# Chunked attention on one core: scores and the product with values side by side on TensorE, the output projection one step earlier

## The chip, the cores and the metric

The kernel runs on one core of one Trainium2 chip. The metric is the device time of one execution in microseconds (us). The kernel before took 1947.82 us, the median of 3 runs (1942.81 to 1955.28). The other seven cores do nothing.

## What is computed

The context `ctx` (32 batches of 256 channels by 2048 tokens) is projected into queries, keys and values, all three from the same tensor. Attention stays inside chunks of 64 tokens, with 8 heads of 32 channels. Then come the output projection, the mask, the residual `x` and a normalisation over the 2048 tokens of each channel:

```
qh, kh, vh = proj(ctx, W)                     # heads of 32, chunks of 64
scores = qh . kh * scale (+ NEG where masked)
attn   = softmax(scores)                      # over the 64 keys of the chunk
out    = (attn . vh) @ W_out.T + b_out
out    = out.transpose * masks + x
out    = (out - mean) * rsqrt(var + 1e-5)     # over the 2048 tokens
```

All arithmetic is float32. The large projections split each operand into a high and a low part (`ctx_hi`, `ctx_lo`, `w_hi`, `w_lo`) and add three products.

## The kernel before, in words

A *block* is 512 tokens of a batch, so there are 4 blocks in a batch and 128 in all. Each of five engines runs its own program, written out by hand: a function `step(p)` with p counting up, in which each operation works on a block at a fixed distance from p. So block p+2 is projected while block p+1 has its scores made, block p-1 is multiplied with the values and block p-2 goes through the output projection. Engines meet only at semaphores. Within an engine everything runs in the written order; an instruction that waits holds up all that stands behind it.

For one block the work is:

- SP (the queue that issues all DMAs) loads `ctx_raw` (four buffers), `mask_all` (six) and `x_raw` (two).
- ACT makes `ctx_hi` (`split_ctx`, L458), POOL `ctx_lo` (`low_ctx`, L565).
- TensorE projects keys, queries (`project_k`, `project_q`, L313) and values (`project_v`, L347), each in two halves that use the two banks of `proj_bank` in turn. ACT empties the banks (`keys` L500, `queries` L491, `values` L508). All projections, the output's too, share these two banks, so each half waits until the half before it in its bank is out.
- POOL turns the mask into rows of 0 or a large negative number (`masked_keys`, L587), and ACT lays them into the four score banks (`lay_negatives`, L470, two halves). Only when both halves lie there may the scores of the block be added on top.
- TensorE makes the scores with 128 matmuls of 32 rows by 64 columns (`scores`, L386). DVE takes the row maximum (L646) and subtracts it (L650, into `prob`, which frees the score banks). ACT takes the exponentials in two halves (L478), DVE sums them (L657) and takes reciprocals (L665), POOL multiplies (`divide`, L557, two halves).
- DVE turns the probabilities in 32x32 squares in one instruction (`turn`, L673), and SP puts them in place with eight DMAs of 128 KB (`move_probs`, L256). These eight wait for the whole turn. TensorE multiplies by the values with 128 matmuls of 64 rows by 32 columns (`probs_times_v`, L419).
- ACT and DVE split the attention output (`high_attention` L485, `low_attention` L680), TensorE projects it (`project_out`, L370, two halves), DVE adds bias and multiplies by the mask (`output`, L691), POOL adds `x` (`add_residual`, L575), DVE takes statistics (L700), and after four blocks the batch is normalised by ACT and POOL and stored.

The order inside a step on TensorE is: scores(p+1), keys(p+2), queries(p+2), first half of the output projection (p-2), product with values (p-1), second half of the output projection (p-2), values(p+2).

Of the kernel before, what the change touches and what calls it, by code (L numbers as in the profile page):

```python
# [14 lines left out]
HALVES = C // P  # L15
ROWS = P // DH
BLOCK = 512
BLOCKS = T // BLOCK
# [32 lines left out]
def attention_kernel(nc, x, ctx_in, mask, w_in_t, b_in, w_out_t, b_out, out):  # L51
    stack = ExitStack()
    with stack:
# [110 lines left out]
        def there(n):  # L164
            return 0 <= n < ALL
# [15 lines left out]
        def periods(step):  # L181
            for p in range(-3, ALL + 4):
                step(p)

        @block.sync
        def _(sp):
# [85 lines left out]
            def step(p):  # L272

                move_values(p + 1)
                if p >= -2:
                    load_ctx(p + 6)
                if there(p + 2):
                    sp.wait_ge(q_proj, 2 * (p + 2) + 1)
                if p >= -1:
                    load_mask(p + 3)  # L280
                if there(p + 2):
                    sp.wait_ge(q_proj, 2 * (p + 2) + 2)
                if p >= 3:
                    load_x(p - 1)
                move_probs(p)

                if p == ALL + 2:
                    for n in range(p - 7, ALL):
                        store(n)
                elif p < ALL + 2:  # L290
                    store(p - 7)

# [6 lines left out]
        def _(pe):  # L299
# [16 lines left out]


            def project_k(n, f):
                if not there(n):
                    return  # L320
                if f == 0:
                    pe.wait_ge(ctx_hi_done, 2 * (n + 1))
                    pe.wait_ge(ctx_lo_done, 2 * (n + 1) - 1)
                    if n == 0:
                        pe.wait_ge(ctx_lo_first, 1)
                wait(pe, v_f_done, 2 * (n - 1) + f + 1 if n else 0)
                project_qk(n, f, k_proj, C)
# [7 lines left out]
            def project_v(n, f):  # L335
                if not there(n):
                    return
                if there(n - 4):
                    pe.wait_ge(y_done, 2 * (n - 4) + f + 1)
                else:  # L340
                    pe.wait_ge(q_f_done, 2 * n + f + 1)
                for t in range(2):
# [9 lines left out]
            def project_out(m, f):  # L352
                if not there(m):
                    return
                if f == 0:
                    if m == 0:
                        pe.wait_ge(dve_const, 5)
                    pe.wait_ge(o_hi_done, m + 1)
                if there(m + 4):
                    pe.wait_ge(q_f_done, 2 * (m + 4) + f + 1)  # L360
                elif there(m + 3):
# [11 lines left out]

            def scores(n):
# [5 lines left out]
                pe.wait_ge(seeded, 2 * (n + 1))  # L380
                for c in range(CPB):
# [20 lines left out]

            def probs_times_v(n):
                if not there(n):
# [6 lines left out]
                wait(pe, o_lo_done, n)  # L411
                pe.wait_ge(moved[n % MOVES], 128 * (n // MOVES + 1))
                for c in range(CPB):
                    for r in range(ROWS):
# [17 lines left out]
            def step(p):  # L432
                met(PIECE_WAITS)
                scores(p + 1)
                project_k(p + 2, 0)
                project_k(p + 2, 1)
                project_q(p + 2, 0)
                project_q(p + 2, 1)
                if p == -1:
                    output_bias()  # L440
                project_out(p - 2, 0)
                probs_times_v(p - 1)
                project_out(p - 2, 1)
                project_v(p + 2, 0)
                project_v(p + 2, 1)

            periods(step)

        @block.scalar
        def _(act):  # L450
# [71 lines left out]

            def step(p):
                keys(p + 2, 0)
                split_ctx(p + 3, 0)
                keys(p + 2, 1)
                split_ctx(p + 3, 1)
                queries(p + 2, 0)
                queries(p + 2, 1)
                exponentials(p + 1, 0)  # L530
                exponentials(p + 1, 1)
                lay_negatives(p + 2, 0)
                lay_negatives(p + 2, 1)
                high_attention(p - 1)
                values(p + 2, 0)
                if p == ALL + 2:
                    for n in range(p - 7, ALL):
                        normalise(n)
                elif p < ALL + 2:
                    normalise(p - 7)  # L540
                values(p + 2, 1)

# [3 lines left out]
        def _(pool):  # L546
# [54 lines left out]
            def step(p):  # L601
                if p < 0:
                    masked_keys(p + 2)
                low_ctx(p + 3, 0)
                low_ctx(p + 3, 1)
                if p >= 0:
                    masked_keys(p + 2)
                if p < ALL + 2:
                    normalise(p - 7)
                if there(p - 3) and (p - 3) % BLOCKS == BLOCKS - 1:  # L610
                    reciprocal_std((p - 3) // BLOCKS)
                if p == ALL + 2:
                    for n in range(p - 7, ALL):
# [9 lines left out]
        def _(dve):  # L623
# [103 lines left out]
            def step(p):  # L727
                less_maximum(p + 1)
                if p == -1:
                    output_bias()  # L730
                turn(p)
                statistics(p - 3)
                done = there(p - 3) and (p - 3) % BLOCKS == BLOCKS - 1
                if done:
                    mean_and_variance((p - 3) // BLOCKS)
                output(p - 2, 0)
                sum_up(p + 1, 0)
                output(p - 2, 1)
                sum_up(p + 1, 1)
                reciprocals(p + 1)  # L740
                low_attention(p - 1)
                if done:
                    mean_shift((p - 3) // BLOCKS)
                if p == ALL + 2:
                    normalise_last()
# [25 lines left out]
```

## Time and profile before

| what | value |
|---|---|
| median of 3 runs | 1947.82 us |
| profiled execution, span from first to last instruction | 1939.0 us |
| TensorE matmul busy | 1891.7 us, 98% |
| DVE busy | 1703.2 us, 88% |
| POOL busy | 1504.6 us, 78% |
| ACT busy | 1330.1 us, 69% |
| mean granted clock of TensorE | 0.991 |
| DMA engines, share of the span (main queue) | 74.2% |

The device time of the profiled execution itself is not listed apart from its span; the median of the three runs lies 8.8 us above that span. Times in the trace are counted from the start of the span. A row of the timeline gives the start and the length of an instruction (or of several merged, with x2 and so on), the engine, the line in the kernel and the tile it writes. In the chain of waits a row is a stretch of time and the work that filled it.

### The profile page before, as it was taken

How to read it: one execution, taken by the hardware profiler on the slowest of the kernel's cores; microseconds unless marked ns; L12 is line 12 of the kernel's file. 1: busy time of each engine (PE TensorE's matmuls, PEld its weight loads, DVE VectorE, ACT ScalarE, POOL GpSimd, SP SyncE). 2: the span in 40 equal slices, each digit the busy share in tenths (PEclk: the TensorE clock that was granted, in tenths of full speed). 3: DMA queues.
4: the chain of work that ended last, by engine and by line, in shares of the span. 5: the costliest groups of instructions: out<-in, count | busy, mean ns of one | idle time of the engine just before them, and what ended most of it. 6: DMA issues, size and time to landing. Idle time of an engine off the chain costs nothing.

```text
span 1939.0 us, 90624 instructions
## 1 busy us (share of the span) xinstructions
PE 1891.7 (98%) x40488; PEld 1608.1 (83%) x40488; DVE 1703.2 (88%) x1577; ACT 1330.1 (69%) x1792; POOL 1504.6 (78%) x1059
## 2 busy tenths in 40 slices
PE   7999999999999999999999999999999999999994
PEld 6888888888888888888888888888888888888882
DVE  4898889899999978998988999888899889989986
ACT  5667667767767766776777677677667767767762
POOL 4677778878888778878777887787778778778874
PEclk9999999999999999999999999999999999999997
DMA  5667778777777767777777777777777777777766
GB/s 171 159 181 215 218 206 224 215 218 223 212 220 222 213 196 217 222 215 215 221 219 212 221 222 214 222 210 215 212 221 219 215 217 216 222 209 222 208 176 195
DMA packets 242882, 409.60 MB, mean 211 GB/s; under 512 B 28992, under 2 KB 94784, under 8 KB 242496
## 3 DMA queue, kind: packets, MB, share of 16 engines
q1 hardware_dynamic: 242496, 403.82, 74.2%
q8 instruction: 320, 5.24, 1.2%
q14 instruction: 66, 0.54, 0.1%
HBM read 168.82 MB, written 67.11 MB: 122 GB/s over the span
## 4 chain that ended last, share of the span: by engine, by line
PE 96%; DVE 1%; issue 1%; ACT 1%; DMA 0%; POOL 0%; SPq 0%; DVEq 0%
PE proj_bank L313 38%; PE proj_bank L370 19%; PE proj_bank L347 19%; PE score_bank L386 11%; PE o_bank L419 9%; DMA b_cols<-b_in 0%; ACT prob L478 0%; ACT score_bank L470 0%; DVE squares L673 0%; SPq L256 0%; POOL prob L557 0%; DVE stats L700 0%; POOL y L575 0%; DMA prob_t<-squares 0%; DVE sums L657 0%
## 5 line engine op out<-in xcount | busy, mean ns | idle before, releaser
L557 POOL TENSOR_TENSOR prob<-prob,recip 128x1024 f32<-128x1024 f32 x256 | 482.0, 1904 | 46.5 <-DVE recip L665 46.5
L575 POOL TENSOR_TENSOR y<-y,x_raw 128x512 f32<-128x512 f32 x256 | 331.5, 1295 | 181.1 <-DVE y L691 181.1
L565 POOL TENSOR_TENSOR ctx_lo<-ctx_raw,ctx_hi 128x512 fp32r<-128x512 f32 x255 | 330.2, 1295 | 171.9 <-ACT ctx_hi L458 159.7
L500 ACT ACTIVATE k_f<-proj_bank,b_cols 128x512 f32<-128x512 f32 x256 | 176.4, 689 | 365.2 <-PE proj_bank L313 365.2
L646 DVE TENSOR_REDUCE row_max<-score_bank 128x32 f32<-128x2048 f32 x128 | 293.4, 2292 | 138.7 <-PE score_bank L386 138.7
L313 PE MATMUL proj_bank<-ctx_hi,w_hi 128*128 128x512 f32 x1024 | 337.1, 410 | 3.0 <-DVE ctx_lo L630 3.0
L313 PE MATMUL proj_bank<-ctx_hi,w_lo 128*128 128x512 f32 x1024 | 322.1, 396 | 0.7 <-issue 0.7
L313 PE MATMUL proj_bank<-ctx_lo,w_hi 128*128 128x512 f32 x1024 | 322.1, 396 | 0.0
L657 DVE TENSOR_REDUCE sums<-prob 128x16 f32<-128x1024 f32 x256 | 309.3, 1209 | 5.0 <-ACT prob L478 5.0
L650 DVE TENSOR_TENSOR prob<-score_bank,row_max 128x2048 f32<-128x2048 f32 x128 | 293.3, 2292 | 4.4
L673 DVE STREAM_TRANSPOSE squares<-prob 128x2048 f32<-128x2048 f32 x128 | 294.6, 2301 | 2.6 <-POOL prob L557 2.6
L478 ACT ACTIVATE prob<-prob 128x1024 f32<-128x1024 f32 x256 | 255.2, 1047 | 5.6 <-DVE prob L650 5.6
L491 ACT ACTIVATE q_f<-proj_bank,b_cols 128x512 f32<-128x512 f32 x256 | 176.4, 689 | 115.1 <-PE proj_bank L313 115.1
L470 ACT ACTIVATE score_bank<-neg_rows 128x1024 f32<-128x1024 f32 x256 | 251.3, 1016 | 0.0
L587 POOL TENSOR_SCALAR neg_rows<-mask_all 128x512 f32<-128x512 f32 x128 | 247.0, 1929 | 2.5 <-DMA mask_all<-mask 2.5
L691 DVE SCALAR_TENSOR_TENSOR y<-proj_bank,b_final,mask_all 128x512 f32<-128x512 f32 x256 | 190.3, 744 | 49.8 <-PE proj_bank L370 49.8
L313 PEld LDWEIGHTS proj_bank<-ctx_hi,w_lo 128*128 128x128 f32 x1024 | 194.0, 189 | 46.9 <-issue 1.0
L313 PEld LDWEIGHTS proj_bank<-ctx_lo,w_hi 128*128 128x128 f32 x1024 | 193.5, 189 | 45.2
L313 PEld LDWEIGHTS proj_bank<-ctx_hi,w_hi 128*128 128x128 f32 x1024 | 183.9, 189 | 46.5 <-issue 3.7
L386 PE MATMUL score_bank<-k_f,q_f 32*64 32x64 f32 x16384 | 214.7, 233 | 3.0 <-ACT score_bank L470 2.8
L386 PEld LDWEIGHTS score_bank<-k_f,q_f 32*64 32x64 f32 x16384 | 196.7, 130 | 21.3 <-issue 3.8
L419 PEld LDWEIGHTS o_bank<-prob_t,v_f 64*32 64x32 f32 x8192 | 169.8, 105 | 51.2 <-issue 51.2
(45 smaller groups left out, 3487.1 us busy)
## 6 DMA issues: line engine op xcount, KB each, us to landing
prob_t<-squares SPq DMA_DIRECT2D x1024, 128.0 KB
ctx_raw<-ctx SPq DMA_DIRECT2D x128, 512.0 KB, 4.8
x_raw<-x SPq DMA_DIRECT2D x128, 512.0 KB, 4.8
out<-y SPq DMA_DIRECT2D x128, 512.0 KB, 4.3
mask_all<-mask SPq DMA_DIRECT2D x128, 256.0 KB, 4.2
v_x<-v_f SPq DMA_DIRECT2D x256, 128.0 KB, 3.4
y<-w_in_t SPq DMA_DIRECT2D x1, 768.0 KB, 5.6
y<-w_out_t SPq DMA_DIRECT2D x1, 256.0 KB, 6.7
```

Source lines behind the costliest of these rows:

```text
L313: last = pe.matmul(proj_bank[:, f, :], w[:, h, col + f * P:col + (f + 1) * P], c[:, n % 2, h, :], start=(a == 0 and h == 0), stop=(a == 2 ...
L347: last = pe.matmul(proj_bank[:, f, t * C:(t + 1) * C], c[:, n % 2, h, tok:tok + P], w[:, h, 2 * C:3 * C], start=(a == 0 and h == 0), stop= ...
L370: last = pe.matmul(proj_bank[:, f, :], w[:, h, f * P:(f + 1) * P], o[:, m % 2, :, h, :], start=(a == 0 and h == 0), stop=(a == 2 and h == 1))
L386: last = pe.matmul(score_bank[f * CHUNK:(f + 1) * CHUNK, r, tokens], q_f[head, n % 2, f, tokens], k_f[head, n % 2, f, tokens], start=False ...
L419: last = pe.matmul(o_bank[r * DH:(r + 1) * DH, f, c * CHUNK:(c + 1) * CHUNK], values, prob_t[keys, :, r * CPB + c, :], start=True, stop=Tr ...
L557: pool.tensor_tensor(part, part, half(slots(recip[:, n % 2, :]), i), ALU.mult).then_inc(norm_done, 1)
L565: pool.tensor_tensor(ctx_lo[:, n % 2, :, tokens], ctx_raw[:, n % BLOCKS, :, tokens], ctx_hi[:, n % 2, :, tokens].bitcast(F32), ALU.subtrac ...
L575: pool.tensor_tensor(part, part, x_raw[:, m % 2, f, :], ALU.add).then_inc(added, 1)
L646: dve.tensor_reduce(row_max[:, :].rearrange("p (r c) -> p r c", c=CPB), scores_of, AX_X, ALU.max).then_inc(max_done, 1)
L650: dve.tensor_tensor(prob[:, n % 2, :, :, :], scores_of, slots(row_max[:, :]), ALU.subtract).then_inc(less_done, 1)
L657: dve.tensor_reduce(sums[:, i * SLOTS // 2:(i + 1) * SLOTS // 2], half(prob[:, n % 2, :, :, :], i).rearrange("p r c k -> p (r c) k"), AX_X ...
L673: dve.transpose(squares[:, :, :, :], prob[:, n % 2, :, :, :].rearrange("p r c (b j) -> p b (r c) j", j=SQ)).then_inc(turned, 1)
```

## The change

No instruction of arithmetic is added or removed; the steps are arranged anew.

- TensorE: one group of waits at the head of a step (context, queries and keys and laid rows, moved probabilities), then scores(p+1), product with values(p-1), keys(p+2), queries(p+2), values(p+2), and both halves of the output projection, now of block p-1. The banks are waited for accordingly.
- ACT: splitting of the context and of the attention output first; the first half of the mask rows is laid before the queries and exponentials, the second half after the values.
- POOL: the residual is added at the head of the step, ahead of `low_ctx` and `masked_keys`.
- DVE: `low_attention` right behind `turn`; the output of block p-1 at the end, behind the reciprocals.
- SP: the store first, then context, the eight moves, x, the values' move, the mask.
- The turn stays one instruction, and the eight moves still wait for all of it; only their order among themselves differs. Two steps at the end go.

```diff
         def periods(step):
-            for p in range(-3, ALL + 4):
+            for p in range(-3, ALL + 2):
                 step(p)
...
             def move_probs(n):
-                sp.wait_ge(turned, n + 1)
-                wait(sp, pv_done, n)
-                for f in range(HALVES):
-                    for a in range(2):
-                        for b in range(2):
+                wait(sp, pv_done, n)
+                sp.wait_ge(turned, n + 1)
+                for b in range(2):
+                    for f in range(HALVES):
+                        for a in range(2):
...
             def step(p):                       # SP
-                move_values(p + 1)
+                store(p - 7)
+                if there(p + 2):
+                    sp.wait_ge(k_proj, 2 * (p + 2) + 1)
                 if p >= -2:
                     load_ctx(p + 6)
-                if there(p + 2):
-                    sp.wait_ge(q_proj, 2 * (p + 2) + 1)
+                move_probs(p)
+                if p >= 3:
+                    load_x(p - 1)
+                move_values(p + 2)
                 if p >= -1:
                     load_mask(p + 3)
-                if there(p + 2):
-                    sp.wait_ge(q_proj, 2 * (p + 2) + 2)
-                if p >= 3:
-                    load_x(p - 1)
-                move_probs(p)
...
             def step(p):                       # TensorE
                 met(PIECE_WAITS)
+                context_ready(p + 2)
+                rows_ready(p + 1)
+                probs_ready(p - 1)
                 scores(p + 1)
+                probs_times_v(p - 1)
                 project_k(p + 2, 0)
                 project_k(p + 2, 1)
                 project_q(p + 2, 0)
                 project_q(p + 2, 1)
                 if p == -1:
                     output_bias()
-                project_out(p - 2, 0)
-                probs_times_v(p - 1)
-                project_out(p - 2, 1)
                 project_v(p + 2, 0)
                 project_v(p + 2, 1)
+                project_out(p - 1, 0)
+                project_out(p - 1, 1)
...
             def step(p):                       # ACT
+                split_ctx(p + 3, 0)
+                split_ctx(p + 3, 1)
+                high_attention(p - 1)
                 keys(p + 2, 0)
-                split_ctx(p + 3, 0)
                 keys(p + 2, 1)
-                split_ctx(p + 3, 1)
+                lay_negatives(p + 2, 0)
                 queries(p + 2, 0)
+                exponentials(p + 1, 0)
                 queries(p + 2, 1)
-                exponentials(p + 1, 0)
                 exponentials(p + 1, 1)
-                lay_negatives(p + 2, 0)
+                values(p + 2, 0)
+                values(p + 2, 1)
                 lay_negatives(p + 2, 1)
-                high_attention(p - 1)
-                values(p + 2, 0)
...
             def step(p):                       # POOL
                 if p < 0:
                     masked_keys(p + 2)
+                add_residual(p - 2, 0)
+                add_residual(p - 2, 1)
                 low_ctx(p + 3, 0)
                 low_ctx(p + 3, 1)
                 if p >= 0:
                     masked_keys(p + 2)
...
-                add_residual(p - 2, 0)
-                add_residual(p - 2, 1)
                 divide(p + 1, 0)
                 divide(p + 1, 1)
...
                 turn(p)                        # DVE
-                statistics(p - 3)
+                low_attention(p - 1)
+                statistics(p - 2)
...
-                output(p - 2, 0)
                 sum_up(p + 1, 0)
-                output(p - 2, 1)
                 sum_up(p + 1, 1)
                 reciprocals(p + 1)
-                low_attention(p - 1)
+                output(p - 1, 0)
...
+                output(p - 1, 1)
```

What a step of ACT looks like in the middle of the program, before (lines of the kernel before; `k_f`, `q_f`, `v_f` are keys, queries, values taken out of `proj_bank`):

```order
L500 ACTIVATE k_f<-proj_bank,b_cols 128x512 [waits rows_done,k_proj]
L458 ACTIVATE ctx_hi<-ctx_raw 128x2x256 [waits v_proj,ctx_loaded3]
L500 ACTIVATE k_f<-proj_bank,b_cols 128x512 [waits rows_done,k_proj]
L458 ACTIVATE ctx_hi<-ctx_raw 128x2x256
L491 ACTIVATE q_f<-proj_bank,b_cols 128x512 [waits q_proj] x2
L478 ACTIVATE prob<-prob 128x1024 [waits less_done] x2
L470 ACTIVATE score_bank<-neg_rows 128x1024 [waits less_done,neg_done]
L470 ACTIVATE score_bank<-neg_rows 128x1024
L485 ACTIVATE o_hi<-o_bank 128x1024 [waits out_proj,pv_done]
```

and the same stretch now:

```order
L491 ACTIVATE o_hi<-o_bank 128x1024 [waits out_proj,pv_done]
L506 ACTIVATE k_f<-proj_bank,b_cols 128x512 [waits rows_done,k_proj] x2
L476 ACTIVATE score_bank<-neg_rows 128x1024 [waits less_done,neg_done]
L497 ACTIVATE q_f<-proj_bank,b_cols 128x512 [waits q_proj]
L484 ACTIVATE prob<-prob 128x1024 [waits less_done]
L497 ACTIVATE q_f<-proj_bank,b_cols 128x512 [waits q_proj]
L484 ACTIVATE prob<-prob 128x1024 [waits less_done]
L514 ACTIVATE v_f<-proj_bank 128x512 [waits pv_done,v_proj] x2
L476 ACTIVATE score_bank<-neg_rows 128x1024
```

The first laying of the mask rows, with its wait for POOL (`neg_done`), has moved ahead of both queries and both exponentials. POOL's step, before:

```order
L565 TENSOR_TENSOR ctx_lo<-ctx_raw,ctx_hi 128x2x256 [waits ctx_hi_done] x2
L587 TENSOR_SCALAR neg_rows<-mask_all 128x512 [waits seeded,mask_loaded4]
L598 TENSOR_SCALAR y<-y,rstd,shift 128x512
L575 TENSOR_TENSOR y<-y,x_raw 128x512 [waits x_loaded0,y_done]
L575 TENSOR_TENSOR y<-y,x_raw 128x512 [waits y_done]
L557 TENSOR_TENSOR prob<-prob,recip 128x1024 [waits recip_done]
```

and now:

```order
L563 TENSOR_TENSOR prob<-prob,recip 128x1024
L581 TENSOR_TENSOR y<-y,x_raw 128x512 [waits x_loaded0,y_done]
L581 TENSOR_TENSOR y<-y,x_raw 128x512 [waits y_done]
L571 TENSOR_TENSOR ctx_lo<-ctx_raw,ctx_hi 128x2x256 [waits ctx_hi_done] x2
L593 TENSOR_SCALAR neg_rows<-mask_all 128x512 [waits seeded,mask_loaded4]
L604 TENSOR_SCALAR y<-y,rstd,shift 128x512
```

The two additions of the residual now stand between the division and the mask rows. On SP a step now reads:

```order
L230 DMA out<-y 128x2x512 [waits z_done1,z_done0]
L194 DMA ctx_raw<-ctx 128x2x512 [waits ctx_lo_done,k_proj]
L256 DMA prob_t<-squares 32x1024 [waits turned,pv_done]
L256 DMA prob_t<-squares 32x1024 x7
L211 DMA x_raw<-x 128x2x512 [waits added]
L241 DMA v_x<-v_f 64x4x128 [waits pv_done,v_f_done]
L241 DMA v_x<-v_f 64x4x128
L203 DMA mask_all<-mask 128x512 [waits y_done]
```

The load of x, which stood ahead of the eight moves, is behind them.

## Rows read from the trace of the kernel before

**Rows 1.** Chain of waits, one step of TensorE: start us, us, what.
```profile
915.84 2.88 PE proj_bank L347 x24
918.72 1.59 PE score_bank L386 x92
920.30 5.77 PE proj_bank L313 x24
926.07 1.40 PE proj_bank L370 x6
927.48 1.41 PE o_bank L419 x91
928.89 1.58 PE proj_bank L370 x6
```

**Rows 2.** Timeline of DVE: start us, us, engine line operation tiles.
```profile
916.55 1.21 DVE L657 TENSOR_REDUCE sums<-prob 128x16 f32<-128x1024 f32 x1
917.86 0.35 DVE L665 RECIPROCAL recip<-sums 128x32 f32<-128x32 f32 x1
...
924.87 2.30 DVE L673 STREAM_TRANSPOSE squares<-prob 128x2048 f32<-128x2048 f32 x1
```

**Rows 3.** Timeline of ACT.
```profile
911.48 0.69 ACT L491 ACTIVATE q_f<-proj_bank,b_cols 128x512 f32<-128x512 f32 x1 [0.71 <-PE proj_bank L313]
912.06 2.00 ACT L478 ACTIVATE prob<-prob 128x1024 f32<-128x1024 f32 x2
913.96 1.96 ACT L470 ACTIVATE score_bank<-neg_rows 128x1024 f32<-128x1024 f32 x2
...
917.31 0.60 ACT L508 ACTIVATE v_f<-proj_bank 128x512 f32<-128x512 f32 x1 [0.44 <-PE proj_bank L347]
```

**Rows 4.** Timeline of POOL.
```profile
918.29 3.77 POOL L557 TENSOR_TENSOR prob<-prob,recip 128x1024 f32<-128x1024 f32 x2 [0.28 <-DVE recip L665]
923.22 2.67 POOL L565 TENSOR_TENSOR ctx_lo<-ctx_raw,ctx_hi 128x512 fp32r<-128x512 f32 x2 [1.17 <-ACT ctx_hi L458]
925.86 1.92 POOL L587 TENSOR_SCALAR neg_rows<-mask_all 128x512 f32<-128x512 f32 x1
...
929.08 1.29 POOL L575 TENSOR_TENSOR y<-y,x_raw 128x512 f32<-128x512 f32 x1 [0.54 <-DVE y L691]
```

**Rows 5.** Chain of waits at the end, last eight moves: first, last with landing, the product.
```profile
1909.42 0.51 SPq L256
...
1913.78 2.44 DMA prob_t<-squares
...
1916.35 1.67 PE o_bank L419 x96
```

**Rows 6.** Timeline of SP, the eight moves in the middle of the run.
```profile
928.97 6.20 SPq L256 DMA_DIRECT2D prob_t<-squares  x8
```

**Rows 7.** The page, DMA issues: KB each, us to landing.
```profile
x_raw<-x SPq DMA_DIRECT2D x128, 512.0 KB, 4.8
```

**Rows 8.** Chain of waits, two stretches in which TensorE stood still.
```profile
262.44 1.64 issue
...
703.69 2.60 issue
...
706.77 2.86 PE proj_bank L370 x6
```

**Rows 9.** Busy time by stretch: PE, PEld, DVE, ACT, POOL busy, clock, DMA share, GB/s.
```profile
265.00:266.00 1.00, 1.00 (x7) 0.83 (x6) 0.00 (x0) 0.56 (x1) 0.00 (x0) 1.00 0.32 74
...
706.00:707.00 1.00, 0.70 (x18) 0.53 (x18) 0.00 (x0) 0.13 (x1) 0.00 (x0) 0.50 0.04 16
...
712.00:713.00 1.00, 1.00 (x8) 1.00 (x8) 1.00 (x2) 0.77 (x2) 0.92 (x1) 0.76 0.85 197
```

**Rows 10.** Chain of waits: the scores of block 3, and those of block 127.
```profile
61.66 1.75 PE score_bank L386 x86
...
1888.91 1.59 PE score_bank L386 x93
```

More of the change, by code:

```diff
@@ L315, in project_qk, with context_ready @@
                 last.then_inc(proj, 1)
+            def context_ready(n):
+                if not there(n):
+                    return
+                pe.wait_ge(ctx_hi_done, 2 * (n + 1))
+                pe.wait_ge(ctx_lo_done, 2 * (n + 1) - 1)
+                if n == 0:
+                    pe.wait_ge(ctx_lo_first, 1)
             def project_k(n, f):
@@ L320, in project_k @@
                     return
[L321 to L326, printed above, removed]
+                if there(n - 4):
+                    pe.wait_ge(y_done, 2 * (n - 4) + f + 1)
+                else:
+                    wait(pe, v_f_done, 2 * (n - 1) + f + 1 if n else 0)
                 project_qk(n, f, k_proj, C)
@@ L337, in project_v @@
                     return
[L338 to L341, printed above, removed]
+                pe.wait_ge(q_f_done, 2 * n + f + 1)
                 for t in range(2):
@@ L358, in project_out @@
                     pe.wait_ge(o_hi_done, m + 1)
-                if there(m + 4):
-                    pe.wait_ge(q_f_done, 2 * (m + 4) + f + 1)
-                elif there(m + 3):
+                if there(m + 3):
                     pe.wait_ge(v_f_done, 2 * (m + 3) + f + 1)
@@ L372, in project_out, with rows_ready @@
                 last.then_inc(out_proj, 1)
-            def scores(n):
+            def rows_ready(n):
                 if not there(n):
@@ L380, in scores @@
                 pe.wait_ge(seeded, 2 * (n + 1))
+            def scores(n):
+                if not there(n):
+                    return
                 for c in range(CPB):
@@ L401, in open_banks, with probs_ready @@
                 last.then_inc(opened, 1)
-            def probs_times_v(n):
+            def probs_ready(n):
                 if not there(n):
@@ L412, in probs_times_v @@
                 pe.wait_ge(moved[n % MOVES], 128 * (n // MOVES + 1))
+            def probs_times_v(n):
+                if not there(n):
+                    return
                 for c in range(CPB):
@@ L523, in step @@
             def step(p):
+                split_ctx(p + 3, 0)
+                split_ctx(p + 3, 1)
+                high_attention(p - 1)
                 keys(p + 2, 0)
-                split_ctx(p + 3, 0)
                 keys(p + 2, 1)
-                split_ctx(p + 3, 1)
+                lay_negatives(p + 2, 0)
                 queries(p + 2, 0)
+                exponentials(p + 1, 0)
                 queries(p + 2, 1)
-                exponentials(p + 1, 0)
                 exponentials(p + 1, 1)
-                lay_negatives(p + 2, 0)
+                values(p + 2, 0)
+                values(p + 2, 1)
                 lay_negatives(p + 2, 1)
-                high_attention(p - 1)
-                values(p + 2, 0)
-                if p == ALL + 2:
-                    for n in range(p - 7, ALL):
+                if p == ALL + 1:
+                    for n in range(p - 6, ALL):
                         normalise(n)
-                elif p < ALL + 2:
-                    normalise(p - 7)
-                values(p + 2, 1)
+                else:
+                    normalise(p - 6)
             periods(step)
@@ L607, in step @@
                     masked_keys(p + 2)
[L608 to L613, printed above, removed]
+                if p < ALL + 1:
+                    normalise(p - 6)
+                if there(p - 2) and (p - 2) % BLOCKS == BLOCKS - 1:
+                    reciprocal_std((p - 2) // BLOCKS)
+                if p == ALL + 1:
+                    for n in range(p - 6, ALL):
                         normalise(n)
-                add_residual(p - 2, 0)
-                add_residual(p - 2, 1)
                 divide(p + 1, 0)
```

14 lines of the change are left out of this document (6 added, 8 removed).

## The prediction, made before the changed kernel was run

> **What bounds the kernel now.** I read the chain of waits first. In the middle of the run it never leaves TensorE: one step is values 2.88, scores 1.59, keys and queries 5.77, first half of the output projection 1.40, product with values 1.41, second half 1.58, in all 14.63 us without a gap [rows 1]. From the scores of block 3 to those of block 127 lie 124 steps and 1888.91 - 61.66 = 1827.25 us, so 14.74 a step [rows 10]; the 0.11 above 14.63 is a handful of stalls such as those of [rows 8]. What is left is 61.7 us ahead of them and 1939.0 - 1888.9 = 50.1 us behind. The timelines of the other engines come next, because the change rearranges who waits for whom: the reader should see there how long each link is.
>
> **TensorE's own work.** The step now has one stretch of small tiles instead of two. Re-entering the large matmuls costs 1.58 - 1.40 = 0.18 us [rows 1], and one of the two entries goes: 14.63 - 0.18 = 14.45. No row shows scores directly followed by the product with values; that seam costs between 0 (they are both small tiles) and about 0.18 (as dear as the entry seen). I take 0; it won't decide. The Trainium skill, TensorEngine Tiling (Array Packing), section Key Properties, says that a change of tiling mode drains the array; scores (32 by 64) to product (64 by 32) is such a change, and by it the sum would be 14.6 instead of 14.45. If nothing else waited, 124 steps would save 0.18 x 124 = 22 us.
>
> **Something else waits.** Three loops close once a step, through the other engines.
>
> *Loop of the mask rows.* POOL now does, in order: divide, two residual additions, `ctx_lo`, mask rows. ACT may not take out the queries or do the exponentials until it has laid the first half of those mask rows, and the exponentials lead back to the next division. From the end of the mask rows (call it M): laying one half 0.98 (1.96 for two), queries 0.58 to the next start, exponential 0.95 (913.96 - 912.06 = 1.90 for two), queries 0.58, exponential 1.00 [rows 3]; the second sum to its reciprocal 1.31, reciprocal to division 0.43 [rows 2, 4]; division 3.77, two additions 2.58, `ctx_lo` 2.67, mask rows 1.92 [rows 4]. Sum 16.77; two crossings between engines that these starts don't hold, about 0.05 each by the 0.08 between reciprocal and division, make 16.9 us. Before, the laying stood behind the exponentials, so the loop wasn't closed.
>
> *Where TensorE stands in it.* It reaches the values' projection at 1.59 + 1.41 + 5.77 = 8.8 us of its step [rows 1], but bank 0 is free only at M + 0.05 + 0.98 + 0.69 = M + 1.7. Values start there, the first half of the output projection at M + 4.8 (the values' bank is emptied after the second exponential, 4.15 + 0.60 [rows 3]), and the step ends at M + 4.8 + 2.8 = M + 7.6. With a step of 16.9, M lies at 16.9 - 7.6 = 9.3 and TensorE stands still from 8.8 to 11.0: 2.2 us in every step.
>
> *Loop of the moves.* From the start of the scores to the end of the turn took 927.17 - 918.72 = 8.45 us [rows 1, 2]; that order is unchanged on DVE. From the first of eight issues to the product that needed them it was 1916.35 - 1909.42 = 6.93 us when little else moved [rows 5]. Now the scores of the next step stand behind the same wait, so a step takes at least 8.45 + 6.93 = 15.4 us. Before, the product came later in the step and the moves were issued over a step early; nothing waited.
>
> *Loop of x.* Its load now follows the eight moves: 8.45, eight issues 5.0 (4.36 / 7 = 0.62 each) [rows 5], landing 4.8 [rows 7], two additions, `ctx_lo`, mask rows 7.2, then 7.6 to the end of a step. That is 33.1 us over two steps, 16.5 each. It is just short of the first loop, so whatever delays the scores soon delays x and with it M.
>
> **What the standstill does to the clock.** After 2.60 us of standstill, which began at 703.69, the granted clock was 0.50 at 706 and came back in the course of 712 [rows 8, 9]: 1.2 GHz instead of 2.4 for at least 6.5 us. Six large matmuls took 2.86 there against 1.40 to 1.58 [rows 1, 8]. After 1.64 us at 262 it stayed at 1.00 [rows 8, 9]. A standstill of 2.2 lies between the two, so I count it as even odds. If the clock falls, values and half of the output projection run at half speed and the step ends at M + 10.5 instead of M + 7.6, as 6.5 us at half speed lose about 3.3, of which 0.4 lay in waits between the halves. The end of the outputs then holds up POOL's additions by some 0.5. The next step has M 6.9 after its start and no standstill at the values, but its head waits for the moves (15.4), and its x lands 8.45 + 5.0 + 4.8 = 18.2 after its start where POOL is through with its division at 6.9 + 9.6 = 16.5 (M + 5.9 to the reciprocal by the links above, and 3.77): 1.7 more. Two steps are then 2 x 16.9 + 0.5 + 1.7 = 36.0, or 18.0 each, and the standstill that follows is 2.2 + 0.7 = 2.9, long enough to drop the clock again. So once it falls it keeps falling every second step. The Trainium skill, TensorE: Matmul & The Clock Gate, section HAM oscillation, describes this pattern, a wait in every round that puts the clock down each time; the row at 706 agrees for one wait, none here shows it repeated.
>
> **The sum.** I take the pairs with a fallen clock for three quarters of the steps and 16.9 for the rest: 0.75 x 18.0 + 0.25 x 16.9 = 17.7 us. The head: two early steps get longer by about 4 in all (scores of blocks 1 to 3 at 15.5 apart), 65.7. The tail keeps its chain of division, turn, moves, product, output and normalisation; a step fewer and one late output less may save up to 3, I keep 50.1. Together 65.7 + 50.1 + 124 x 17.7 = 2311 us of span. The median lay 8.8 above the span of the profiled execution, so 2320 us. In short, time = 125 + 124 x step. Splitting, keys, statistics and the store are moved too; all have over 1 us of slack beside a step of 17 and cost nothing, as DVE is busy 1703.2 / 128 = 13.3 us a step and ACT 1330.1 / 128 = 10.4. If POOL's loop were gone, DVE would be the one with little to spare.
>
> **Rivals.**
> - *The clock holds* (the 2.2 us behave like the 1.64): step 16.9, 125 + 2096 = 2221 us. For it: 2.2 is only 0.56 longer than a standstill that left the clock alone. Against: one fall is enough to make the next standstill 2.9 long. Chance 0.24.
> - *Moves and x cost more.* In the middle of the run the eight issues took 6.20 us rather than 5.0 [rows 6]. 1.2 more on x in every late step gives (36.0 + 1.2) / 2 = 18.6, and 2431 us; falls in each step would do the same. For it: the DMA engines were busy 74% of the span, and the moves end in a landing like any other. Against: in the new order little else is in flight during the moves. Chance 0.13.
> - *Only the moves bind.* If the mask rows come early enough, because part of POOL's work is shorter in company than the rows say, the step is 15.4, up to 16.4 with the 6.20: 2035 to 2160 us. It decides only if the mask-row loop shrinks by 1.5 us of 16.9. Chance 0.11.
> - *Faster than before.* The seam saved is real; it shows if the moves land within TensorE's own 14.45 us, that is if turn to product takes 14.45 - 8.45 = 6.0 instead of 6.93, and if ACT's laying isn't held (loop under 14.45, 2.4 below my sum). Then 61.7 + 50.1 + 8.8 + 124 x 14.45 = 1912 us. Against: each link of both loops is a measured length. Chance 0.04, 0.01 of it within 1% of the time before.
>
> **Chances and range.** Forecast case (step 17.2 to 18.1) 0.48. The range reaches from 2195, below the clock that holds, to 2425, the upper bound of the moves; it leaves out the last two rivals and a part of the dear moves. About 1% is what a measurement of this kernel can tell from no change. Slower by over 1% 0.96, within 1% 0.01, faster 0.03.
>
> **What would show it.** In the profile after: TensorE's busy share falls to some 85%; the first large wait on it is at the values' projection, on the queries taken out by ACT; ACT waits at L476 for POOL's mask rows; POOL is nearly without gaps from division to mask rows, and waits only for the reciprocals, with some wait for x; the granted clock has a mean of 0.8 to 0.9. If TensorE instead waits at the head of the step for the moves and nowhere else, the loop of the mask rows was overrated and the step is 15.4 to 16.4. If the step is 14.5, both loops were.

## The result, and the profile after

The changed kernel takes 2720.77 us (median of 4 runs, 2695.01 to 2730.98) against 1951.55 of the kernel before (4 runs): a ratio of 1.393, interval 1.387 to 1.399. The forecast was 2320, with a range up to 2425. The direction was right, the size was not: a step takes 20.98 us (scores of block 3 at 73.55, of block 127 at 2674.88, 124 steps) instead of the 17.7 forecast.

The page of the profile after, busy time by engine, the clock by slice, the queue that brings instructions, and the chain by engine:

```profile
PE 2156.2 (79%) x40488; PEld 1796.8 (66%) x40488; DVE 1756.9 (65%) x1577; ACT 1303.7 (48%) x1792; POOL 1472.0 (54%) x1059
...
PEclk8888888878888888888887888888898888888886
...
q8 instruction: 320, 5.24, 0.8%
...
PE 71%; issue 20%; DMA 4%; SPq 3%; DVE 1%; POOL 1%; ACT 0%; DVEq 0%; ACTq 0%
```

TensorE's busy share fell from 98% to 79%, and a fifth of the chain is "issue": time in which the engine waited for nothing that the profile shows. The head of one step of that chain and the whole of the next, where [rows 1] had a step without a gap (start us, us, what; lines of the changed kernel: 385 scores, 422 product, 308 keys and queries, 345 values, 366 output):

```profile
1306.59 1.52 PE score_bank L385 x91
1308.11 0.17 PE o_bank L422
1308.28 2.61 issue
1310.89 2.04 PE o_bank L422 x121
1312.93 0.72 PE proj_bank L308
1313.65 0.98 issue
1314.63 6.75 PE proj_bank L308 x23
...
1327.09 1.58 PE score_bank L385 x84
1328.67 0.79 PE o_bank L422 x53
1329.46 3.40 issue
1332.86 0.85 PE o_bank L422 x53
1333.70 7.32 PE proj_bank L308 x24
1341.02 2.84 PE proj_bank L345 x24
1343.87 2.78 PE proj_bank L366 x12
1346.65 1.52 PE score_bank L385 x91
```

The rows show a stop *inside* the product. It is not at the seam with the scores and not at the head of the step. It begins 0.17 us after the product's first matmul in one step and 0.79 in the next, and the two alternate through the run. By the records of the product in these stretches, 1 and 65 of the 128 matmuls had run. The step with the early stop has another one, of 0.98 us here, behind the first matmul of the keys, which is exactly 128 matmuls further on. The second step adds up: 19.56 us = 14.38 of work at full speed, 3.40 of stop, 1.55 more for keys and queries than their 5.77 in [rows 1], and 0.23 by which the product's two parts exceed 1.41. The 1.55 is the clock:

```profile
1332.00:1333.00 1.00, 0.14 (x18) 0.14 (x25) 1.00 (x1) 0.00 (x0) 1.00 (x2) 1.00 0.00 0
...
1334.00:1335.00 1.00, 1.00 (x5) 0.82 (x4) 1.00 (x1) 0.77 (x1) 1.00 (x2) 0.74 0.00 0
1335.00:1336.00 1.00, 1.00 (x4) 0.81 (x3) 1.00 (x2) 0.10 (x1) 1.00 (x1) 0.50 0.00 0
```

(busy time of PE, PEld, DVE, ACT, POOL, then granted clock, DMA share and GB/s, as in [rows 9]). After the standstill the clock goes to 0.50, 1.2 GHz. Over the run its mean is 0.84. The waits of the whole run, engine, line, what for, total us, times, longest:

```profile
ACT o_hi L491 <- PE o_bank L422: 853.9, 128, 9.0
PE o_bank L422 <- issue: 444.2, 126, 5.1
PE proj_bank L308 <- issue: 77.0, 63, 2.1
PE score_bank L385 <- DMA prob_t<-squares: 6.7, 17, 1.1
ACT score_bank L476 <- POOL neg_rows L593: 2.1, 1, 2.1
PE proj_bank L345 <- ACT q_f L497: 1.7, 1, 1.7
```

The stop comes in 126 of 128 products, 3.5 us each. What the prediction put first, ACT waiting for the mask rows and TensorE for the queries, is next to nothing: 2.1 and 1.7 us. For the moves TensorE waited 6.7 us at the scores.

### The profile page after: what moved, and what is told of

The parts are those of the page before. It is cut to its first block, busy times and chain, and to the rows that moved or that the text cites. A ratio compares the mean times of both kernels' runs of the same rounds, so it can differ in the third digit from the quotient of the medians.

```text
span 2723.3 us, 90494 instructions
## 1 busy us (share of the span) xinstructions
PE 2156.2 (79%) x40488; PEld 1796.8 (66%) x40488; DVE 1756.9 (65%) x1577; ACT 1303.7 (48%) x1792; POOL 1472.0 (54%) x1059
## 3 DMA queue, kind: packets, MB, share of 16 engines
q8 instruction: 320, 5.24, 0.8%
## 4 chain that ended last, share of the span: by engine, by line
PE 71%; issue 20%; DMA 4%; SPq 3%; DVE 1%; POOL 1%; ACT 0%; DVEq 0%; ACTq 0%
PE proj_bank L308 32%; PE proj_bank L345 12%; PE proj_bank L366 11%; PE o_bank L422 9%; PE score_bank L385 7%; DMA prob_t<-squares 3%; SPq L256 3%; POOL prob L563 0%; DVE squares L679 0%; DVE row_max L652 0%; SPq L194 0%; DMA b_cols<-b_in 0%; ACT score_bank L476 0%; DVE sums L663 0%; POOL ctx_lo L571 0%
## 5 line engine op out<-in xcount | busy, mean ns | idle before, releaser
L422 PE MATMUL o_bank<-prob_t,v_f 64*32 64x64 f32 x8192 | 260.7, 270 | 445.8 <-issue 441.9
L491 ACT ACTIVATE o_hi<-o_bank 128x1024 fp32r<-128x1024 f32 x128 | 131.0, 1023 | 853.9 <-PE o_bank L422 853.9
L308 PE MATMUL proj_bank<-ctx_hi,w_hi 128*128 128x512 f32 x1024 | 444.3, 512 | 79.9 <-issue 77.0
L422 PEld LDWEIGHTS o_bank<-prob_t,v_x 64*32 64x32 f32 x8192 | 199.6, 126 | 460.5 <-issue 460.5
L308 PE MATMUL proj_bank<-ctx_hi,w_lo 128*128 128x512 f32 x1024 | 397.6, 476 | 0.0
L308 PE MATMUL proj_bank<-ctx_lo,w_hi 128*128 128x512 f32 x1024 | 384.7, 462 | 0.0
L308 PEld LDWEIGHTS proj_bank<-ctx_hi,w_lo 128*128 128x128 f32 x1024 | 248.3, 242 | 156.8 <-issue 94.3
L308 PEld LDWEIGHTS proj_bank<-ctx_hi,w_hi 128*128 128x128 f32 x1024 | 242.5, 251 | 72.7 <-issue 21.5
L308 PEld LDWEIGHTS proj_bank<-ctx_lo,w_hi 128*128 128x128 f32 x1024 | 240.2, 235 | 63.6
L422 PE MATMUL o_bank<-prob_t,v_x 64*32 64x64 f32 x8192 | 241.5, 271 | 2.4 <-issue 2.4
```

Of the source, the lines that this page charges most:

```text
L308: last = pe.matmul(proj_bank[:, f, :], w[:, h, col + f * P:col + (f + 1) * P], c[:, n % 2, h, :], start=(a == 0 and h == 0), stop=(a == 2 ...
L422: last = pe.matmul(o_bank[r * DH:(r + 1) * DH, f, c * CHUNK:(c + 1) * CHUNK], values, prob_t[keys, :, r * CPB + c, :], start=True, stop=Tr ...
```

## The experiments

**Theory S**: scores and product in a row are 256 small matmuls and 256 weight loads in some 3 us. TensorE uses up its instructions faster than they arrive and stands still until the next piece of the program is there. The page has 320 packets and 5.24 MB of instructions on q8, 16.4 KB each. TensorE executes 2 x 40488 = 80976 matmuls and loads, 253 for each of those packets, so I take a piece as 256 instructions; the rest would be its waits for semaphores. That the stops of two neighbouring steps lie 64 matmuls, or 128 instructions, apart fits a step of 640 instructions: 320 packets for 128 steps are two and a half in each. **Rivals**: the moves of the probabilities (M), the change of tile shape at the seam (T), and the prediction's loops as the only cost.

The trace of the changed kernel also has the times of those packets. Set beside the stops of the chain above, with the times at which TensorE went on:

| packet of q8 lands | TensorE goes on | later by |
|---|---|---|
| 1309.75 | 1310.89 | 1.14 us |
| 1313.21 | 1314.63 | 1.42 us |
| 1331.38 | 1332.86 | 1.48 us |

So it is in the whole run: of the 189 stops over 0.5 us behind the start of the program, 188 end 1.0 to 1.7 us after such a packet has landed, with a median of 1.39, though there is a packet only every 8.5 us. The same holds for the four stops in the kernel before (1.33 to 1.51). That TensorE stood still until a piece of its program had come is thus shown, and the experiments show what makes the pieces late.

### One part alone: the product behind the scores, in the kernel before

```diff
                 scores(p + 1)
+                probs_times_v(p - 1)
                 project_k(p + 2, 0)
...
                 project_out(p - 2, 0)
-                probs_times_v(p - 1)
```

> The kernel before with one thing changed: on TensorE the product with values(p-1) stands right behind scores(p+1). Theory S (supply of instructions): 128 + 128 small matmuls with their 256 weight loads in a row use up TensorE's instructions faster than they arrive; it stops for 1.5 to 4.5 us inside the product in every step, the granted clock falls behind it, step 18.5 to 20.5 us, 2400 to 2650 us. Theory M (moves): nothing but the earlier need for the eight moves counts (turn to landing), step 15.4 to 16.5, 2030 to 2170 us, and the wait stands at the product's first matmul with the moves as releaser. Theory T (seam): a stop at the seam between 32*64 and 64*32 tiles, at the product's first matmul, the same in each step.

Measured 2557.5 us (e1), ratio 1.308 (1.289 to 1.326). The time is that of theory S, its mechanism is not in the rows:

```profile
PE o_bank L419 <- DMA prob_t<-squares: 404.7, 127, 5.1
...
1330.89 0.37 SPq L211
...
1336.09 5.30 DMA prob_t<-squares
1341.38 0.14 issue
1341.52 2.18 PE o_bank L419 x127
```

TensorE waits at the product's first matmul for the moves, 3.2 us in 127 steps. SP issues these only behind the load of x, which in the old order waits for the second half of the queries; the moves then land 5.3 us after the last issue. So this is M's place, at 19.3 us for this step (the product before began at 1322.20) where M said at most 16.5. The run shows that the adjacency alone costs 31% in the old surroundings. It says nothing on stops for instructions, which that wait would hide.

### Keys between scores and product, in the changed kernel

```diff
                 scores(p + 1)
-                probs_times_v(p - 1)
                 project_k(p + 2, 0)
                 project_k(p + 2, 1)
+                probs_times_v(p - 1)
...
-                high_attention(p - 1)
                 keys(p + 2, 0)
                 keys(p + 2, 1)
+                high_attention(p - 1)
```

> The changed kernel with the two key projections (12 + 12 instructions, 2.9 us) put between scores and product, and ACT's split of the attention output behind the keys. Theory S: the stops inside the product are gone or under 1 us, and what is left is the loop of the mask rows of the prediction: step 16.9 to 18.0, 2220 to 2360 us. Theory M: the wait for the moves is untouched, still 2650 to 2730 us. Theory T: two more seams with large tiles, 0.2 us each, and the stop gone with the seam, also 2220 to 2360: e4 tells it from S.

Measured 2271.0 us (e2), ratio 1.161 (1.156 to 1.167): 450 us came back from moving one group by 2.9 us. Its chain is the loop of x of the prediction, link by link:

```profile
1345.37 2.31 DVE squares L679
...
1353.22 5.30 DMA x_raw<-x
...
1361.18 2.48 POOL ctx_lo L571 x2
1363.66 1.90 POOL neg_rows L593
...
1367.27 3.23 PE proj_bank L345 x24
```

Between the turn and the landing lie the eight issues. Stops remain, but 188 us in 120 waits instead of 528 in 190 (all waits of PE's matmuls put down to "issue").

### Keys and queries between

The edit is the same with both queries ahead of the product too; ACT splits the attention output behind the exponentials, DVE behind the reciprocals.

> As e2, but keys and queries (5.8 us of large matmuls) between scores and product, and the attention output split behind the exponentials on ACT and behind the reciprocals on DVE. Theory S: no stop at all inside the product, step 16.9 to 18.0 by the loop of the mask rows, 2220 to 2360 us, at most 2% from e2. Theory M: 2650 us or more.

Measured 2479.6 us (e3), ratio 1.268 (1.259 to 1.277). A miss: stops fell further, to 90 us in 64 waits, but the product now comes 5.8 us later, the moves wait for it (`pv_done`), x waits behind the moves, and the loop of x is 18.8 us a step (scores at 1308.45 and, two steps on, at 1346.05). The stops are only one of the costs.

### The same program, 64 idle waits fewer at its head

```diff
-LEAD = 102
+LEAD = 38
```

> The changed kernel with 38 instead of 102 idle waits at the head of TensorE's program (64 instructions fewer, nothing else). In the changed kernel the stop begins 0.17 us behind the product's first matmul in one step and 0.79 in the next. Theory S: pieces of the program now end 64 instructions later in the work, so the stop begins some 0.35 us later, at 0.5 and 1.1 us; time 2650 to 2780 us. Theories M and T: the stop has nothing to do with the place in the program, it begins at 0.17 and 0.79 as before, time within 1%.

Measured 2565.9 us (e4): 5.7% less than the changed kernel, for removing waits that run once. It fell below the expected time. The chain of this run, one stop of each kind:

```profile
1334.78 0.97 PE o_bank L422 x64
1335.74 4.23 issue
...
1356.15 0.28 PE o_bank L422 x17
1356.43 4.64 issue
```

The stops begin behind 17 and 81 matmuls instead of 1 and 65. The distance of 64 stays and both have moved by 16 matmuls, 32 instructions. I had expected 64, or 0.35 us. The other runs with a changed LEAD agree that two idle waits count as one instruction: 64 fewer move the stop of the kernel before from behind matmul 111 of the product to behind 127 (e10 below), and 36 more move it by 9 matmuls between e14 and e13. That the place moves at all excludes T and M, which know nothing of the place in the program. What became cheaper is mainly the stop behind the first matmul of the keys: 77.0 us in 63 waits in the changed kernel, 2.4 in one wait here, while the stops in the product still take 419.5 of 444.2.

### The load on the DMA engines

```diff
-                sp.dma_start(out[... all 256 rows of the block ...])
+                sp.dma_start(out[bass.ds(batch, 1), 0:1, j * BLOCK:(j + 1) * BLOCK]...)
...
+                rows = P if n < MASKS else 1
-                sp.dma_start(mask_all[:, n % MASKS, :], ...)
+                sp.dma_start(mask_all[0:rows, n % MASKS, :], ...)
```

> The changed kernel without most of the two transfers that SP issues just ahead of the burst: the store of the result writes 2 KB instead of 512 KB per block, and masks behind the first six blocks load one row instead of 128 (the output is left out except for one row of each block). Everything else waits as before. Theory C (the pieces of TensorE's program queue behind the transfers on the same DMA engines): the stop inside the product shrinks from 3.6 us in the mean to under 2, time 2350 to 2520 us. Theory L (a piece simply takes long): the stop stays at 3.3 to 3.8 us and the time within 3% of the changed kernel.

Measured 2478.2 us (e5), 8.9% less than the changed kernel. The stops:

```profile
PE o_bank L423 <- issue: 263.4, 126, 3.6
```

That is 2.09 us each against 3.53, a little over the 2 I had named. Pieces of the program come later when the DMA engines are loaded. The packets themselves take as long as before (median 1.08 us against 0.98), and TensorE goes on as long after they land (1.39 in both), so it is their start that comes later. More than half of the stop stays without these two transfers.

### The mask rows late, x early, and both

```diff
-                lay_negatives(p + 2, 0)      # rows late: ahead of the queries ...
+                lay_negatives(p + 2, 0)      # ... now behind exponentials(p + 1, 1)
...
+                    load_x(p - 1)            # x early: ahead of ...
                 move_probs(p)
-                    load_x(p - 1)            # ... not behind
```

> e2 with the first laying of the mask rows back behind the exponentials on ACT. Theory of the prediction's loops: the loop of the mask rows is open, and the loop of x with it, as x only leads to the next step through those rows: step 14.8 to 15.8, 1960 to 2085 us. Rival (x alone sets the step of e2): 2230 us or more.

> e2 with the load of x issued ahead of the eight moves, nothing else. Prediction's loops: the loop of x is gone, that of the mask rows (16.9 us a step) stays, 2190 to 2240 us. Rival (x alone sets the step): below 2100 us.

> e6 and e7 together, with 38 idle waits at the head of TensorE's program. Loops open, fewer stops for instructions: step 14.6 to 15.3, 1935 to 2020 us, within 3% of the kernel before on either side.

Measured 2345.2 (e6, rows late), 2199.9 (e7, x early) and 2233.9 us (e8, both). x early met its forecast: the loop of x is gone and what stays is the loop of the mask rows. In its chain the rows of one step are done at 1354.09 and those of the next at 1370.66, 16.57 us apart where the forecast had 16.9, and the steps take 16.6. Rows late was 3% slower than e2, not 10% faster, and both together missed 1935 to 2020 by far. The chain of rows late never reaches POOL, so that loop is open. It runs through ACT instead, because I had put the laying ahead of `values` and the output projection waits for the values' bank; but TensorE is hardly held by that:

```profile
PE proj_bank L308 <- issue: 161.2, 63, 4.2
PE o_bank L422 <- issue: 69.0, 55, 2.5
PE proj_bank L366 <- ACT v_f L514: 64.7, 125, 0.5
```

The wait for ACT is 0.5 us a step. The stops for instructions are 237 us in all, against 188 in e2, and the mean clock is 0.946 against 0.972. In e8 they are 158 us. So e6 and e8 don't show what the loop of the mask rows alone was worth: with it open, the stops fill most of what it left.

### All loops opened

Keys and queries between, x early, both mask rows laid last, attention output split between exponentials and values, LEAD 58 (e9). Then the same with the wait for the moves at the product (e12), and e12 with other numbers of idle waits (e13, e14):

```diff
-                probs_ready(p - 1)       # e9: at the head of the step
                 scores(p + 1)
...
+                probs_ready(p - 1)       # e12
                 probs_times_v(p - 1)
...
-LEAD = 58                                # e9, e12
+LEAD = 138                               # e13; 102 in e14
```

> The changed kernel with keys and queries between scores and product (bursts of small matmuls evenly spaced, 5.8 and 5.7 us of large ones between them), x loaded ahead of the moves, both mask rows laid last on ACT, the attention output split between exponentials and values, and 58 idle waits at the head of TensorE's program. Theory S with the three loops: no loop is closed under 14.6 us and hardly a stop is left, step 14.6 to 15.0, 1935 to 1985 us, within 2% of the kernel before, perhaps 3 us below it for the shorter tail. Rival (the prediction's loops were not the whole: something else of the changed order costs): above 2050 us.

> e9 with the wait for the moved probabilities standing right ahead of the product instead of at the head of the step. In e9 the chain goes scores 1.58, keys and queries 5.78, product 1.43, eight issues and their landing 7.4, then the next scores: 16.3 us. Theory (this loop set e9, as its product stands 5.8 us later): with the wait at the product the loop is open, step 14.6 to 15.2, 1935 to 2010 us. Rival (stops for instructions and the clock set e9): still above 2200 us.

> e12 with 138 idle waits at the head of TensorE's program instead of 58. In e12 every second step has a stop behind 114 of the 128 matmuls of the product (mean 3 us, and the clock falls behind the long ones), the others take 14.66. If the place of the piece's end decides: with the end 14 instructions ahead of the scores no piece lies in a burst alone, hardly a stop is left, step 14.6 to 15.1, 1945 to 2005 us. If the place doesn't matter, 2180 to 2240 us as e12.

> e12 with 102 idle waits, as in the changed kernel: a piece then ends one matmul behind the scores, as seen there. If the place decides, the stops move to the first key matmul and there are none in the product; as the piece before it is used up in 1.5 us, they stay at 1 to 3 us in every second step: 1990 to 2130 us, between e13 and e12. If it doesn't matter, 2180 to 2240 us.

Measured 2327.7 (e9, ratio 1.198), 2211.4 (e12, 1.129), 2162.5 (e13, 1.105) and 2085.9 us (e14, 1.066). e9 missed, for a wait left at the head: its chain is scores 1.58, keys and queries 5.78, product 1.43, eight issues, landing 2.32, next scores, 16.3 us; stops and clock bring the mean step to 17.8. With that wait moved, e12's chain holds TensorE alone:

```profile
1324.72 1.59 PE score_bank L385 x87
1326.31 5.79 PE proj_bank L308 x24
1332.10 1.41 PE o_bank L422 x91
1333.51 3.05 PE proj_bank L345 x24
1336.56 2.78 PE proj_bank L366 x12
1339.35 1.68 PE score_bank L385 x94
...
1348.12 5.25 issue
...
1353.83 5.21 PE proj_bank L345 x24
```

One step takes 14.6 us, as TensorE's own work says. The next has a stop of 5.25 us and a values' projection at half clock, 5.21 for 3.05. So the 13% over the kernel before are stops and clock, with next to nothing else. The three values of LEAD move the stop from the product (58) into the scores (138) and to the first key matmuls (102), with a total of 197, 159 and 118 us. I had expected 138 to be the best and nearly free of stops. That was wrong, as was the forecast for e12; e14 lies in its range. None of the three matches the kernel before.

### The place and the load, in the kernel before

The old order with LEAD 38 (e10), and that with the light DMA of e5 (e15).

> The kernel before with 38 idle waits at the head of TensorE's program instead of 102, nothing else. Theory S: its 128 small matmuls in a row come close to using up the pieces on hand, so the place where a piece ends decides: more stops, 1 to 6% slower (1965 to 2070 us), with TensorE waiting for nothing the profile shows inside scores or product. Rival (supply matters only for 512 in a row): the same within 0.5%.

> The kernel before with 38 idle waits (e10, 2064.6 us) and, as in e5, without most of the store and of the mask loads (the output is left out except for one row of each block). If the load on the DMA engines makes pieces late, the stops (98 us in e10, more with the clock's fall) shrink to under half: 1930 to 1995 us. If only the place counts, 2040 to 2080 us.

Measured 2064.6 us (e10), ratio 1.063 (1.055 to 1.071), and 1990.8 (e15), ratio 1.017 (1.011 to 1.023). Waits of TensorE, e10 and then e15:

```profile
PE o_bank L419 <- issue: 98.4, 62, 2.8
```

```profile
PE o_bank L420 <- issue: 41.8, 62, 2.1
```

62 stops in both, behind matmul 127 of the product, where the kernel before has 4 behind matmul 111: the place sets whether there is a stop, the load how long it is (1.59 and 0.67 us). So the kernel before is itself near the limit, and LEAD 102 is part of its speed.

With pieces of 128 matmuls and as many loads one can count back from a stop to the end of the piece before, and see how much work TensorE had had since. This is an estimate from the traces, as piece ends at which nothing stops can't be seen. In the changed kernel it is 1.5 us at both stops in the product, in e11 below the same, in e10 1.6, in e14 2.1, in e13 2.2: a whole piece of nearly nothing but small matmuls, and a stop every time. At the place of the four stops in the kernel before it is 5.2 us, as large matmuls of the queries and of the output lie in that piece; in e10 it begins behind most of them. A burst of 256 small matmuls always contains a whole piece wherever the pieces end, and one of 128 contains nearly a whole one only for some values of LEAD.

### A shorter burst

Every second chunk's scores left out, in the changed kernel.

```diff
-                for c in range(CPB):
+                for c in range(0, CPB, 2):
```

> The changed kernel with every second chunk's scores left out on TensorE (64 matmuls instead of 128; the rest of the softmax runs on what lies in the banks). The burst is 384 instructions instead of 512, and a step 128 instructions shorter. By its work alone this saves 0.76 us a step: 2620 us. Theory S: the step is now a whole number of the 256-instruction pieces, so the stop begins at the same matmul in every step instead of alternating between two places 64 matmuls apart; time 2350 to 2600 us. Theory of a seam or a data wait: two places or none as before, 2620 us or more.

Measured 2287.7 us (e11). A step is now 128 instructions shorter, 512, the page has 256 packets on q8 instead of 320, two for each step, and the stop begins 0.79 us into the product in nearly every step instead of alternating, as whole pieces say:

```profile
1313.39 0.79 PE o_bank L422 x53
1314.17 1.75 issue
...
1331.41 2.56 issue
```

It is 433 us less for 0.76 x 128 = 97 us of work. Waits put down to "issue" fall from 528 to 268 us, and the mean clock rises from 0.84 to 0.93. The time fell below the expected 2350.

## Why the prediction was wrong

- **TensorE's own work, the seam.** This is the step that failed. It priced scores directly followed by the product "between 0 ... and about 0.18" and took 0. Measured, the two in a row cost a stop of 3.5 us in nearly every step, and 1.6 us or more of lower clock behind it: the granted clock fell 122 times in the run. It fell at each of the 107 stops of 2 us and over and at none of the 52 under 1.5. The landings of the packets, e2, e4 and e11 show that it is the burst of small instructions and its place, not the seam. The rows to see it were there: the standstills in [rows 8] are put down to "issue", and both lie inside the product, behind its matmul 111. I had filed them as rare stalls. In the kernel before 4 products in 128 stop; e10 turns that into 62 by moving the program 64 idle waits.
- **The loops of mask rows and x.** Right as mechanisms, but covered: with the step at 21 us POOL is ready early (2.1 us of wait for its rows in the whole run). With the burst split, e2's chain is the loop of x, 2271 us against the prediction's 2221 (steps of 16.9) to some 2357 (of 18.0) for those loops; with x early, e7 gave 2199.9 and a loop of 16.57 against 16.9. In e2 part of that agreement is luck, as it still holds 188 us of stops that the prediction doesn't have.
- **The loop of the moves.** Right that TensorE would not wait for them at length (6.7 us), and the 8.45 us from scores to turn are there (8.40 in the step at 1306.59). One link was left out: SP waits for the first keys before the context load, and the moves stand behind that (1231.8 us of SP's time). With the keys late by the stop, the moves go out 2.4 us after the turn in one of the two steps shown, and 0.8 in the other.
- **The clock.** The number came out by luck: forecast 0.8 to 0.9, measured 0.84, but the standstill behind it was the stop in the product and not the wait for queries, which came to 1.7 us in the whole run. What the Trainium skill describes in TensorE: Matmul & The Clock Gate, section HAM oscillation, a wait in every round that puts the clock down each time, holds here: a standstill in nearly every step and 122 falls of the clock.
- **The drain at a change of tiling mode.** The Trainium skill, TensorEngine Tiling (Array Packing), section Key Properties, says that such a change drains the array. By the 0.18 us of [rows 1] it would have made the step that much longer. In the chain the product follows the scores without a gap (1306.59 + 1.52 = 1308.11), so it explains none of the 3.5 us.
- **Head and tail.** 73.6 and 48.4 us against 65.7 and 50.1. The step accounts for the rest of the miss: 124 times 3.3 us.
- Open: e12, whose stop has 4.1 us of work behind it by the same count, stops in every second step, and the kernel before, with 4.5 at one piece end, doesn't stop there; and how much of the time of a piece is not due to the load, since in e5 2.1 us stay. A version that beats the kernel before was not found.

## What to carry to other kernels

Count instructions, not only microseconds: 128 small matmuls with their 128 weight loads between large ones ran almost unhindered in the kernel before, though not at other places in the program (e10, e12 to e14), and 256 with 256 loads in a row stopped the engine in nearly every step. A standstill of TensorE that the profile puts down to "issue" inside a run of small matmuls, even if it comes four times in a run, told here that the supply was at its limit; adding to the run or shifting the program then cost far more than its work. And before pulling two groups together, follow what the work between them gave time for: waits, landings, and instructions too.

## What the runs showed of the hardware

TensorE stopped at fixed places of its program, 128 instructions apart from step to step with steps of 640, and at one place with steps of 512. Its stops ended 1.0 to 1.7 us after a packet of its program had landed, 188 of 189 in the changed kernel and all four in the kernel before. Removing 64 idle waits that run once at the head changed the time by 5.7% in the changed kernel and by 6.3%, the other way, in the kernel before. Taking away most of two transfers per block, neither of which TensorE waited for, shortened its stops from 3.53 to 2.09 us in the changed kernel and from 1.59 to 0.67 in the kernel before with LEAD 38.
